# Batch 1's 4x4 normalisation moved from the stage before layer 1 into batch 0's attention loop

## What is computed

```
# layer 0 attention, one head of 128: softmax(q k^T * scale) v, then @ Wo + bo
# layer 0 ffn, for each token (n = 4 streams of C = 128):
Z = (x_norm @ W_res.T + H_res_base) / 0.1          # 4x4 for each token
for _ in range(50):                                # "sinkhorn"
    u = -logsumexp(Z + v[..., None, :], axis=-1)
    v = -logsumexp(Z + u[..., :, None], axis=-2)
H_res = (1 - g) * I + g * exp(Z + u[..., :, None] + v[..., None, :])
H_pre, H_post = softmax(...), softmax(...)         # 4 weights each
y = einsum('btnc,btn->btc', x_streams, H_pre) @ W_branch
out = einsum('btij,btjc->btic', H_res, x_streams) + einsum('btc,btn->btnc', y, H_post)
# layer 1: 32 causal heads of 128 (8 key heads) over 1024 tokens, then a gated sum of low-rank experts
```

## Time and profile before

| | |
|---|---|
| median of 3 runs | 2466.7 us (2463.56 to 2467.55) |
| the profiled execution's own time | 2463.85 us |
| its span in the profile | 2461.6 us |
| share of the span that TensorE, VectorE, ScalarE, GpSimd are busy | 91%, 63%, 43%, 41% |
| `layer0_mix` | 90.8 to 330.4 us |
| batch 0's attention | about 478 to 1380 us, 113 us for an iteration |

### The profile page before, as it was taken

How to read it: one execution, slowest core, us unless ns; L and a number is a source line. 1 busy time by engine, 2 the same in 40 slices (tenths; PEclk the granted TensorE clock), 3 DMA queues, 4 the chain that set the end, 5 groups by cost and what they waited for, 6 DMA issues and landing times. The chain is left out here.

```text
span 2461.6 us, 35450 instructions
## 1 busy us (share of the span) xinstructions
PE 2233.0 (91%) x11154; PEld 1814.2 (74%) x11154; DVE 1554.9 (63%) x3685; ACT 1046.4 (43%) x2182; POOL 1012.0 (41%) x1038
## 2 busy tenths in 40 slices
PE   5767449899999999999999796999999999999998
PEld 4633137688888888888887684788888888888886
DVE  4289875466666666666766455566565756566665
ACT  4322213354545444454545232444454545454543
POOL 2644351264545455363634100435262525343341
PEclk9878779899999999999999998999999999999999
DMA  9500035501010101101010434201101010101010
GB/s 341 189 9 1 0 140 209 207 26 66 9 65 9 65 26 48 56 17 56 26 48 1 166 131 185 86 27 43 47 21 51 26 56 13 60 9 60 18 38 31
DMA packets 74003, 164.83 MB, mean 67 GB/s; under 512 B 4704, under 2 KB 38880, under 8 KB 67296
## 3 DMA queue, kind: packets, MB, share of 16 engines
q1 hardware_dynamic: 73504, 162.69, 18.8%
q10 hardware_dynamic: 432, 1.32, 0.1%
HBM read 113.14 MB, written 72.61 MB: 75 GB/s over the span
## 5 line engine op out<-in xcount | busy, mean ns | idle before, releaser
L1521 DVE TENSOR_TENSOR pT<-psum,pT 128x512 fp32r<-128x512 f32 x576 | 387.0, 689 | 282.4 <-ACT pT L1562 281.6
L1474 POOL TENSOR_TENSOR probs_even<-probs_even,rinv 128x1024 f32<-128x1024 f32 (+2 forms) x192 | 241.0, 1255 | 677.5 <-DVE rinv L1512 677.5
L1562 ACT ACTIVATE pT<-psum 128x512 fp32r<-128x512 f32 x576 | 329.2, 596 | 299.1 <-PE psum L1615 299.0
L1507 DVE CUSTOM_DVE_ANT_0 psum<-psum,causal 128x256 f32<-128x256 f32 (+7 forms) x512 | 386.0, 767 | 38.1 <-PE psum L95 33.3
L1474 POOL TENSOR_TENSOR probs_odd<-probs_odd,rinv 128x896 f32<-128x896 f32 (+2 forms) x192 | 198.6, 1042 | 303.0 <-DVE rinv L1512 302.9
L1556 ACT ACTIVATE probs_even<-psum,nmax 128x1024 f32<-128x1024 f32 (+3 forms) x256 | 204.5, 799 | 250.1 <-DVE nmax L1507 246.2
L93 PE MATMUL psum<-keys,q 128*128 128x512 f32 (+3 forms) x768 | 265.6, 346 | 3.7 <-DVE q L1495 2.8
L95 PE MATMUL psum<-keys,q 128*128 128x512 f32 (+3 forms) x768 | 262.0, 341 | 0.0
L94 PE MATMUL psum<-keys,q 128*128 128x512 f32 (+3 forms) x768 | 261.9, 341 | 0.0
L93 PE MATMUL psum<-pT,vals 128*128 128x512 f32 x576 | 256.3, 445 | 3.9
L1556 ACT ACTIVATE probs_odd<-psum,nmax 128x896 f32<-128x896 f32 (+3 forms) x256 | 176.7, 691 | 148.1 <-DVE nmax L1507 145.9
(11 more groups left out here) (272 smaller groups left out, 4410.5 us busy)
## 6 DMA issues: line engine op xcount, KB each, us to landing
k_parts<-kv_out SPq DMA_DIRECT2D x32, 512.0 KB, 4.9
wq<-wq_copy SPq DMA_DIRECT2D x16, 1024.0 KB, 4.8
wo<-wo_copy SPq DMA_DIRECT2D x16, 1024.0 KB, 4.8
v_parts<-kv_out SPq DMA_DIRECT2D x32, 512.0 KB, 3.9
keys<-k_parts SPq DMA_DIRECT2D x32, 512.0 KB, 4.8
vals<-v_parts SPq DMA_DIRECT2D x64, 256.0 KB, 3.1
acc<-in_x SPq DMA_DIRECT2D x4, 1024.0 KB, 12.3
xn_later<-xn SPq DMA_DIRECT2D x1, 2048.0 KB, 14.5
```

What stands on the lines that cost most here:

```text
L1474: pool.tensor_tensor(p, p, rinv[:, u, h:h + 1].to_broadcast([P, (TB - u) * P]), ALU.mult).then_inc(p_ok, 1)
L1507: dve.tensor_tensor_reduce(out=row, in0=row, in1=causal[:, S - n:S], scale=-1.0, scalar=-2 * MASKED, op0=ALU.add, op1=ALU.min, accum_out=n ...
L1521: dve.tensor_tensor(pT[:, n % PT_SLOTS, 1, :], bank[T_BANK + n % 2], f32(pT[:, n % PT_SLOTS, 0, :]), ALU.subtract).then_inc(t_lo, 1)
L1562: act.activation(pT[:, n % PT_SLOTS, 0, :], bank[T_BANK + n % 2], ACT.Copy).then_inc(t_hi, 1)
```

## The change

- `layer0_mix` normalises only batch 0: `Z`, `K` and the factors are 8 tiles long, a part is 4 tiles. The iteration in logarithms is gone; a short `head` (5 instructions on VectorE) takes off the row and the column maxima, ScalarE takes exponentials of the result and of the column maxima, and 100 linear half steps follow. The steps for the stream weights, for the gate and the head for batch 1 stand in `between`. `PER_UNIT` is 27.
- The branch product is done unit by unit, inside the attention: ScalarE makes the 16 weighted streams of a unit (`share`), TensorE sums them at the unit's end (`branch_in`) and multiplies after the next scores (`branch`), ScalarE copies both results.
- The last copies of weights on ScalarE stand behind unit 2, but for one.
- Batch 1's 100 half steps stand in batch 0's attention, at places listed in `pauses` (20 in an iteration, iterations 0 to 5): VectorE sums and inverts there (`factor`), GpSimd multiplies (`scaling`), in one part of 8 tiles. Recentring is in iteration 2, and the finished matrix comes in iteration 5.
- Batch 1's mixing is done in iterations 5, 6 and 7: 3, 3 and 2 tiles, one step behind ("norm", u, 1) and two behind ("norm", u, 2), for u = 3 to 7. The tiles' loads stand elsewhere in SyncE's queue.
- For batch 0, VectorE's and ScalarE's loops over the iterations are unrolled.

```
-        def part_of(x, k):
-            return x[:, k * (NT // PARTS):(k + 1) * (NT // PARTS)]
-        PER_UNIT = 23
+        def part_of(x, k):
+            return x[:, k * (TB // PARTS):(k + 1) * (TB // PARTS)]
+        FIRST_MAX, PER_UNIT = 4, 27
...
-            pool.wait_ge(chain, RW_STEPS)
-            for t in range(NT):
-                pool.tensor_tensor(shares[:, t, :, :], xn[:, t, :].rearrange("p (n c) -> p n c", n=NS),
-                                   rw[:, t, 0, :].unsqueeze(2).to_broadcast([P, NS, D]), ALU.mult).then_inc(xp_ok, 1)
...
+            def share(n):
+                act.wait_ge(chain, RW_DONE)
+                for k in range(UQ):
+                    t = UQ * n + k
+                    for j in range(NS):
+                        act.activation(shares[:, k, j, :], xn[:, t, j * D:(j + 1) * D], ACT.Copy,
+                                       scale=rw[:, t, 0, j:j + 1]).then_inc(xp_ok, 1)
...
+            halves, recentred, mixing_from = 2 * SINKHORN_ITERS, 2, 5
+            pauses = [("qparts", 0), ("qparts", 1), ("norm", 0, 3), ("qparts", 3), ("turn", 0, 3), ("turn", 1, 2), ("turn", 2, 2),
+                      ("turn", 3, 2), ("turn", 3, 4), ("heads", 3), ("turn", 4, 0), ("turn", 4, 2), ("heads", 4), ("turn", 5, 0),
+                      ("turn", 5, 2), ("heads", 5), ("turn", 6, 0), ("max", 7, 2), ("heads", 7), ("add", 7)]
+            tiles_of = {5: (0, 1, 2), 6: (3, 4, 5), 7: (6, 7)}
...
                 sp.wait_ge(q_mm, it * QS + QS)
                 load(wq[:, 1], m.wq_s[g]).then_inc(wq_in, 16)
+                for t in mixed_now[:2]:
+                    later_loads(t + 1)
...
+                for t in mixed_now[2:]:
+                    later_loads(t + 1)
                 sp.wait_ge(s_mm, it * SC + SC)
                 for k in (1, 0):
                     load(keys[:, k, :], keys_of(g, k)).then_inc(k_in, 16)
...
-                        if h == REP - 2 and 2 <= u:
-                            next(beside, None)
-                            next(beside, None)
+                        if mixes_later and it >= mixing_from and u >= 3 and h:
+                            for _ in range(h):
+                                next(beside, None)
+                    if mixes_later and (it, (kind, *arg)) in half_at:
+                        half = half_at[it, (kind, *arg)] + 1
+                        if half not in (2 * LATER_CHUNK, halves):
+                            scaling(half)
...
+            def scaling(half):
+                pool.wait_ge(factor_ok, factors(half))
+                pool.tensor_tensor(T1, m.k1[:], over_rows(m.row1) if half % 2 else over_cols(m.col1), ALU.mult).then_inc(scaled, 1)
...
+            def factor(half):
+                dve.wait_ge(scaled, half + 1)
+                by = T1 if half % 2 == 0 else T1.rearrange("p t i j -> p t j i")
+                dve.tensor_reduce(m.sm1[:], by, AX.X, ALU.add).then_inc(summed, 1)
+                dve.wait_ge(summed, half + 1)
+                dve.reciprocal((m.col1 if half % 2 else m.row1)[:], m.sm1[:]).then_inc(factor_ok, 1)
```

More of the change, by code:

```diff
@@ new lines, in gates, with later_head @@
+            def gates(_):
+                dve.wait_ge(gate_ok, 1)
+                after(dve.tensor_scalar(gate[:, 1:2], gate[:, 1:2], 1.0, None, ALU.add))
+                after(dve.reciprocal(gate[:, 2:3], gate[:, 1:2]))
+                after(dve.tensor_scalar(gate[:, 3:4], gate[:, 2:3], -1.0, 1.0, ALU.mult, ALU.add))
+                assert done == GATE
+            def later_head(_):
+                head(m.z1[:], slice(TB, NT), m.sm1[:], m.lcol1[:])
+                assert done == LATER_HEAD
@@ L551, in _ @@
             dve.wait_ge(mix_ok, 1)
-            mixes = 0
-            last_op = {t: (x1_ok, t + 1) for t in range(NT)}
+            mixes, at = 0, 2 * sum(CHUNKS)
+            ready = {t: (x1_ok, t + 1) for t in range(TB)}
             for k in range(0, TB, 2):
@@ L566, in _ @@
                         mixes += NS
-                        last_op[t] = mixed, mixes
+                        ready[t] = mixed, mixes
+                        for step, unit_tile in between.pop(at, ()):
+                            step(unit_tile)
+                        at += 1
+            assert not between, (at, between)
         @block.scalar
         def _(act):
-            def chain_step(at, out, in_, func):
-                act.wait_ge(chain, at)
-                act.activation(out, in_, func).then_inc(chain_act, 1)
@@ L669, in _ @@
                         if qt == 0:
+                            if unit == 1:
+                                pe.wait_ge(w_in, 32)
+                            branch(unit - 1)
                             pe.wait_ge(p_exp, UQ * unit)
                             turn(0)
+                            pe.wait_ge(y_ok, unit)
                             turn(1)
@@ L1500, in body @@
                     u = arg[0]
+                    if mixes_later and (it, (kind, *arg)) in half_at:
+                        factor(half_at[it, (kind, *arg)])
+                    if mixes_later and (it, kind, *arg) == (recentred, "norm", 0, 3):
+                        recentre()
+                    if mixes_later and (it, kind, *arg) == (mixing_from, "turn", 1, 2):
+                        finish()
                     if kind == "max":
@@ L1535, in _ @@
             dve.wait_ge(causal_ok, 2)
-            with dve.Fori(0, ITERS - 1) as it:
-                body(it, False)
-            body(ITERS - 1, True)
+            if mixes_later:
+                for it in range(ITERS):
+                    body(it, it == ITERS - 1)
+            else:
+                with dve.Fori(0, ITERS - 1) as it:
+                    body(it, False)
+                body(ITERS - 1, True)
         @block.scalar
```

258 lines of the change are left out of this document (153 added, 105 removed).

## The result

The changed kernel takes 2422.1 us (median of 4 runs, 2420.97 to 2427.06) where the kernel before takes 2466.2 (median of 4, 2463.56 to 2467.55): a ratio of 0.9826, interval 0.9809 to 0.9843, so 1.7% less. The prediction was 2417, range 2395 to 2441. The profiled execution took 2421.2 us.

The account below looks back on a forecast made before the run. VectorE's list was taken to bound `layer0_mix`, and TensorE batch 0's attention. Stage -61.2, pairs +1 and mixing +10 make -50.2 us, from 2463.85 to 2414, or 2417 for a median; range 2395 to 2441.

Parts of the forecast that it names:

- The stage: `layer0_mix`, as long as VectorE's list: 178.4 us with 8 of waits, against 239.6 before, giving 61.2 back.
- The ring: Half steps in `layer0_mix`: product, sum, inverse take 0.91 us, above VectorE's own pace of 0.86; 100 take 91.
- A maximum: VectorE's maxima among the half steps of `layer0_mix`: 1.12 us each after 0.1 of idle time, 16 are 17.9.
- VectorE's waits for TensorE and ScalarE: In `layer0_mix`: 2 us for each of 4 units, 8 in all, between 0 and 6 for each.
- Rival 1: TensorE becomes the bound of `layer0_mix`, units still taking 37 us: 16 less gained, 2433; chance 0.15.
- Rival 2: Everything hides: half steps at 0.86, no waits, mixing at 2 us, so 2396; chance 0.12.
- The pairs: Batch 0's attention: 100 pairs of sum and inverse fit into VectorE's waits; 1 us taken, bounds 0 and 68.
- rival 4: Batch 0's attention: the pairs of sum and inverse aren't hidden, all 100 exposed are 68 us: 2485; chance 0.05.
- The mixing: GpSimd's mixing in batch 0's attention: two iterations at 4.5 us, iteration 7 at 1: 10, bounds 2 and 27.
- The stall ahead of ("turn", 7, 0): Iterations 5 and 6 of batch 0's attention: TensorE stalls about 3.1 us as ("norm", 7, 2) ends late.
- The late keys: SyncE sends the next keys only after the last tile is mixed; they land some 1.4 us late for TensorE.
- rival 3: Batch 0's attention: GpSimd's crowded mixing costs its upper bound, by late loads or ports: 17 to 20 more, 2437; chance 0.12.

Follow-up runs that it names:

- e10: Against the changed kernel, GpSimd's product in `layer0_mix` takes two rows of each matrix in place of four (32 elements for 64); 2415.6 us.
- e7: Against the changed kernel, the four additions of a unit in `layer0_mix` stand two half steps later in VectorE's list; 2416.1 us.
- e3: Against the changed kernel, each sum and inverse of batch 1's normalisation in the attention is done twice at the same places; 2433.3 us.
- e9: The changed kernel itself run once more, as a base on the same chip and in the same rounds; 2421.4 us.
- e11: Against the changed kernel, batch 1's mixing steps spread, four behind the last norm of iterations 5 and 6, and additions two half steps later; 2407.0 us.
- e12: As e11, with two of the last iteration's sixteen mixing steps moved into iterations 5 and 6; 2406.4 us.
- e2: Against the changed kernel, the next unit's keys go ahead of the last fresh tile's load in SyncE's queue; 2417.1 us.
- e1: Against the changed kernel, GpSimd's mixing of batch 1 is left out of batch 0's attention, the tiles' loads staying; 2406.2 us.

## Why the prediction was right, and where it was off

**The stage: right, 181 us for 178.4.** The start took 2.2 us (2.4). The ring took 0.94 for 0.91. The first part's rows, which are the ring, have in the mean 297 ns for the product (305 reckoned), 239 for the sum (220), 253 for the inverse (225) and 148 for the gaps (160): the sum and the inverse were taken too short. (The 205 ns above are the mean with the second part's sums of 170.) That is 3 us in 100. A maximum cost 1.15 (1.12). VectorE's waits for TensorE and ScalarE (5.5, 1.3 and 0.3) came to 7.1 of the 8 taken, and from the matrix to the end 48.4 us passed where 43.4 and 4.2 were counted. "The ring is the limit, not VectorE's list" holds between maxima: e10 shortens only the product and the half step follows, and VectorE's wait of 0.12 us is there to be seen. But 0.12 is all the room that the list has, so a maximum or an addition costs nearly its whole length, as reckoned.

**Rival 1, TensorE bounds the stage: wrong.** The clock rose from 0.86 to between 0.90 and 0.95, and e7 took 5 us out of the stage with TensorE's work unchanged. The sign that was named for it, units of 37 us, is a poor one: a unit was reckoned at 31 us and 2 of waits, and the one of 37.1 us has the recentring in it.

**Rival 2, everything hides: wrong.** Half steps stayed at 0.94 for its 0.86, VectorE waited 7.1 us for its 0, and the mixing cost 16 for its 2.

**The pairs: right.** 0.5 us measured, 1 taken. e3 shows that rival 4's mechanism begins only beyond the pair's size: 95 more pairs of 0.65 in iterations 0 to 4 exposed 7.7 us in all, not 62.

**The mixing: right mechanism, too small a size.** The step that failed is "Two iterations at 4.5, iteration 7 at 1: 10". Iterations 5 and 6 cost 9.5 and 7.8, and iteration 7 nothing (1.2 less than before, as TensorE waits less ahead of the turns of u = 5 and 6: 1.81 and 1.33 us for 2.22 and 2.10): 16. The stall ahead of ("turn", 7, 0) was 3.37 and 3.58 for 3.1. The late keys were 3.51 and 2.08 for 1.4: the last tile's mixing ended when predicted, but the fresh tile's load goes into the queue first, so the keys are issued 0.9 us later, and they land 4.9 and 6.4 us after their issue where 4.8 was taken. With 2.17 and 1.91 in e9, this term differs from run to run. What the sum had no term for is the clock: 3.0 and 1.7 us lost at 0.50 after the waits. The result lies a third of the way to rival 3 (17 to 20 us more than 10, by late loads or by the ports); the ports cost nothing that shows in iterations 5 and 6 of the changed kernel, whose sums close without them to 0.5 us. In the last iteration, where TensorE has no next queries to do, they do cost, in e11 and e12 and already in the kernel before.

The sum: predicted -61.2 + 1 + 10, measured -59.4 for the stage's end (58.7 in the stage's own length, and it began 0.7 us earlier) and +16.7 from there to the end of the attention, of which the pairs are 0.5: 42.7 us between the profiled executions (50.2 were predicted), 44.1 between the medians. Of the 7.5 missing, the attention has 5.7 and the stage 1.8.

## What to carry to other kernels

When a stall of TensorE is priced, price the clock after it: in the changed kernel and e2, four of the five waits of over 3 us in iterations 5 and 6 were followed by 3.4 to 6.8 us at half clock. A shorter wait can do it too, as 1.91 us did in e9:

```profile
1226.19 0.50 PE L94 MATMUL psum<-keys,q 128*128 128x512 f32 x1 [1.91 <-DMA keys<-k_parts]
```

```profile
1227.00:1229.00 2.00, 2.00 (x6) 1.54 (x5) 0.44 (x1) 0.00 (x0) 0.00 (x0) 0.52 0.87 355
```

Work for an otherwise idle engine is best put where that engine's next deadline is far, not where it happens to be called; the same 40 steps cost 16 us crowded ahead of norms (the changed kernel less e1) and some 5 spread (the last iteration of e12, 118.7 us for 114.0). The end of a stage that waits for all engines is such a deadline: about half of those 5 us were lost there. Where a queue carries a load that waits for slow work, everything behind it inherits the wait. A ring of two engines in two parts can set the pace while one of them has almost no room left (0.12 us in 0.94 here), and then other work on that engine costs nearly its whole length.

## What had not been expected of the hardware

- A VectorE product from SBUF to SBUF took 1.44 us for 0.42 when a GpSimd addition had begun 0.04 us before (e12 and e1). The prediction weighed such a case, from the 1.51 us in the earlier trace rows; that TensorE already waited for it in the last iteration of the kernel before had not been seen.
- The granted clock went to 0.50 in iteration 5 after the second wait, of 3.51 us; after the first, of 3.37, it had stayed at 1.00. In iteration 6 and in e2 it fell after the first, of 3.58 and 3.44, and in e9 after one of 1.91.
- An inverse of 16 elements took 253 ns in the mean, 353 for 32 and 100 for one: 6.3 ns an element above 16, 10 below.
